# A recurrent layer on one core: the output projection of a turn by seven block products of 64 columns in place of eight, one turn later

## What is computed

```python
Xz = einsum('btc,hc->tbh', X, Wxz) + bxz      # the same for r and h
def step(H, xs):
    Z = sigmoid(xz + H @ Whz.T + bhz)
    R = sigmoid(xr + H @ Whr.T + bhr)
    H_tilda = tanh(xh + R * H @ Whh.T + bhh)
    H_new = Z * H + (1.0 - Z) * H_tilda
    return H_new, H_new @ Whq.T + bhq
out = x + transpose(Ys, (1, 0, 2))
```

## Time and profile before

| | us |
|---|---|
| median of 3 runs | 2182.04 (2181.3 to 2182.8) |
| the profiled execution | 2182.93 |
| its span | 2181.1 |
| PE busy | 2167.1 (99%) |
| DVE busy | 1544.8 (71%) |
| ACT busy | 788.2 (36%) |
| POOL busy | 173.1 (8%) |

### The profile page before, as it was taken

How to read it: one execution, slowest core, us unless ns; L and a number is a source line. 1 busy time by engine, 2 the same in 40 slices (tenths; PEclk the granted TensorE clock), 3 DMA queues, 4 the chain that set the end, 5 groups by cost and what they waited for, 6 DMA issues and landing times.

```text
span 2181.1 us, 180846 instructions
## 1 busy us (share of the span) xinstructions
PE 2167.1 (99%) x78920; PEld 2153.9 (99%) x78920; DVE 1544.8 (71%) x9602; ACT 788.2 (36%) x4611; POOL 173.1 (8%) x519
## 2 busy tenths in 40 slices
PE   8999999999999999999999999999999999999999
PEld 7999999999999999999999999999999999999998
DVE  5677777777777777777777777777777777777776
ACT  2333333333333333333333333333333333333333
POOL 2000000000000000000000000000000000000000
PEclk9999999999999999999999999999999999999999
DMA  4000000000000000000000000001000000000000
GB/s 163 24 27 25 25 25 27 25 25 25 27 25 25 25 26 25 25 25 24 27 24 26 23 28 23 26 23 28 23 26 23 28 23 26 23 28 24 26 23 24
DMA packets 112290, 62.68 MB, mean 29 GB/s; under 512 B 29328, under 2 KB 111376, under 8 KB 111504
## 3 DMA queue, kind: packets, MB, share of 16 engines
q1 hardware_dynamic: 112272, 62.41, 9.7%
HBM read 45.58 MB, written 16.78 MB: 29 GB/s over the span
## 4 chain that ended last, share of the span: by engine, by line
PE 98%; DMA 0%; DVE 0%; issue 0%; ACT 0%; SPq 0%; DVEq 0%
PE gates L307 61%; PE p_bank L272 17%; PE gates L272 11%; PE y_bank L281 10%; DMA wx_u<-in_w_xu 0%; DVE reset_state L568 0%; DVE pre_t L506 0%; DVE t L594 0%; DVE fresh L536 0%; ACT cand L491 0%; ACT r_gate L471 0%; DVE states L542 0%; ACT z_not L474 0%; DVE kept L577 0%; SPq L203 0%
## 5 line engine op out<-in xcount | busy, mean ns | idle before, releaser
L307 PE MATMUL gates<-wh,states 128*16 128x128 f32 x32768 | 1032.8, 273 | 3.9 <-DMA wh<-in_w_hz 2.8
L307 PEld LDWEIGHTS gates<-wh,states 128*16 128x16 f32 x32768 | 938.4, 103 | 12.5 <-DMA wh<-in_w_hz 3.0
L506 DVE STREAM_TRANSPOSE pre_t<-gates 128x32 f32<-128x32 f32 (+2 forms) x3584 | 617.6, 216 | 316.9 <-PE gates L307 275.5
L307 PE MATMUL gates<-wh,reset_state 128*16 128x128 f32 (+1 forms) x16384 | 585.2, 273 | 1.9 <-DVE reset_state L568 1.9
L471 ACT ACTIVATE r_gate<-pre_t 128x16 f32<-128x16 f32 (+1 forms) x1536 | 234.4, 215 | 869.1 <-DVE pre_t L506 869.1
L307 PEld LDWEIGHTS gates<-wh,reset_state 128*16 128x16 f32 (+1 forms) x16384 | 467.4, 103 | 3.4 <-issue 2.6
L272 PE MATMUL p_bank<-t,s 128*32 128x128 f32 (+1 forms) x8184 | 422.9, 287 | 0.0
L281 PE MATMUL y_bank<-wq,states 128*32 128x128 f32 x8192 | 326.2, 273 | 1.5 <-DVE states L542 1.5
L491 ACT ACTIVATE cand<-pre_t 128x16 f32<-128x16 f32 (+1 forms) x1536 | 234.4, 215 | 233.4 <-DVE pre_t L506 233.4
L281 PEld LDWEIGHTS y_bank<-wq,states 128*32 128x32 f32 x8192 | 277.2, 110 | 1.9 <-DVE states L542 1.8
L272 PEld LDWEIGHTS p_bank<-t,s 128*32 128x32 f32 x8184 | 271.1, 110 | 0.9
(11 more groups left out here) (43 smaller groups left out, 1017.0 us busy)
## 6 DMA issues: line engine op xcount, KB each, us to landing
xr<-in_x_t SPq DMA_DIRECT2D x128, 128.0 KB, 2.0
y_io<-in_x_res SPq DMA_DIRECT2D x256, 64.0 KB, 1.7
out<-y_io SPq DMA_DIRECT2D x256, 64.0 KB, 1.6
x_b<-in_x_t SPq DMA_DIRECT2D x128, 32.0 KB, 1.7
wx_v<-in_w_xv SPq DMA_DIRECT2D x1, 1536.0 KB, 6.5
wx_u<-in_w_xu SPq DMA_DIRECT2D x1, 1536.0 KB, 10.3
wh<-in_w_hr SPq DMA_DIRECT2D x1, 1024.0 KB, 11.7
wh<-in_w_hz SPq DMA_DIRECT2D x1, 1024.0 KB, 14.8
```

Of the source, the lines that this page charges most:

```text
L307: mm = nc.tensor.matmul(gate_rows(g, par, slice(Q * j, Q * j + rows)), of, w, start=False, stop=(m == G - 1), skip_group_check=True)
L506: nc.vector.transpose(flat(pre_t[g][:, a:b]), gate_part(g, par, a, b)).then_inc(done, 1)
```

## The change

The output projection of a turn's two pairs is done by seven block products q1 to q7 as well, two quads deep and 64 columns wide (14 quads of 64 columns in place of 8 of 128). They need both pairs of a turn, so they run a turn later, except q1 and q2, which take pair a alone. They need three more things:

- four sums of weights (`wq_sum`), made once by GpSimd in the first turn (`output_sums`);
- four sums of states (`h_sum`), made by DVE at the start of step 0 (`state_sums`);
- copies and sums between parts of `y_bank`, by ACT (`copy_q1`, the copy to `q16`, the copy of `q167`, `fill_q`) and by DVE (`put_y`).

Both `add_y` of the turn before now stand at the start of step 3. `put_va` moves behind Z's transposes, `sum_2`, `sum_3` and `sum_4` of GpSimd go behind `z_turned` in place of `state_ready`. Parts of p1, p5, p6 and p7 move between the gaps, so that each step has 768 columns behind H and 128 ahead of it. Nothing of SP's loop changes. The last turn projects directly, both pairs at its end.

```diff
+        Q16_AT, Q5_AT, Q7_AT, Y_AT = 0, YW, 2 * YW, (3 * YW, 3 * YW + P)
...
+                nc.gpsimd.tensor_tensor(t1, high[:, 0:half], low[:, 0:half], ALU.subtract).then_inc(yt_ready[0], 1)
+                pool.wait_ge(yt_ready[0], 1)
+                nc.gpsimd.tensor_tensor(t2, high[:, half:G], t1, ALU.subtract).then_inc(yt_ready[1], 1)
+                nc.gpsimd.tensor_tensor(t3, high[:, half:G], high[:, 0:half], ALU.subtract).then_inc(yt_ready[2], 1)
+                pool.wait_ge(yt_ready[1], 1)
+                nc.gpsimd.tensor_tensor(t4, low[:, half:G], t2, ALU.subtract).then_inc(yt_ready[3], 1)
...
                     sum_1(i + 1)
-                    pool.wait_ge(state_ready[N - 1], 4 * i + 3)
+                    pool.wait_ge(z_turned, 4 * i + 2)
                     sum_2(i + 1)
+                    pool.wait_ge(z_turned, 4 * i + 3)
+                    sum_3()
+                    pool.wait_ge(z_turned, 4 * i + 4)
                     sum_4(i + 1)
-                    pool.wait_ge(state_ready[N - 1], 4 * i + 4)
-                    sum_3()
...
+            def y_product(at, of, w):
+                for m in range(half):
                     for j in range(G):
+                        mm = nc.tensor.matmul(y_bank[Q * j:Q * (j + 1), at:at + YW], of(m), w(m, j), start=False,
+                                              stop=(m == half - 1), skip_group_check=True)
+                return mm
+            def state(par, part):
+                return lambda m: states[:, par, part * half + m, B:3 * B]
+            def state_sum(n):
+                return lambda m: h_sum[n][:, m, :]
+            def wq_part(part, col):
+                return lambda m, j: wq[:, part * half + m, P * j + col:P * j + col + YW]
+            def wq_of(n):
+                return lambda m, j: wq_sum[n - 1][:, m, YW * j:YW * (j + 1)]
+            def q1():
+                y_product(Q16_AT, state(0, 0), wq_part(0, 0)).then_inc(q1_done, 1)
+            def q2():
+                y_product(Y_AT[0], state(0, 1), wq_part(1, 0)).then_inc(q2_done, 1)
+            def q3():
+                y_product(Y_AT[0] + YW, state_sum(4), wq_part(1, YW)).then_inc(q34_done, 1)
+            def q4():
+                y_product(Y_AT[1], state(1, 1), wq_of(4))
+            def q5():
+                y_product(Q5_AT, state_sum(1), wq_of(1))
+            def q6():
+                y_product(Q16_AT, state_sum(2), wq_of(2)).then_inc(q6_done, 1)
+            def q7():
+                y_product(Q7_AT, state_sum(3), wq_of(3)).then_inc(q57_done, 1)
...
-                    pe.wait_ge(s3_ready, i + 1)
-                    p7(0, WIDE)
+                    pe.wait_ge(yt_ready[3], 1)
+                    pe.wait_ge(ys2_ready, i)
+                    q6()
                 recur(H, i, 0, first)
                 if first:
                     pe.wait_ge(s2_ready, 1)
...
                         p6(m, ALL)
                     pe.wait_ge(p5_filled, 1)
                     for m in range(half):
-                        mm = p5(m)
+                        mm = p5(m, ALL)
                     mm.then_inc(p56_done, 1)
-                    pe.wait_ge(s3_ready, 1)
                     pe.wait_ge(t_ready[2], 1)
-                    p7(0, WIDE)
-                p7(0, NARROW)
+                pe.wait_ge(s3_ready, i + 1)
+                p7(0, ALL)
                 p7(1, ALL).then_inc(p7_done, 1)
                 if not first:
-                    project_y(2 * i - 1, 1, 0, G)
-                recur(R, i, 1)
-                recur(Z, i, 1)
+                    pe.wait_ge(q16_copied, i)
+                    q5()
+                    q7()
                 if not last:
                     pe.wait_ge(xr_loaded, 16 * (i + 2))
                     if first:
                         pe.wait_ge(p16_copied, 1)
                     p1(0, WIDE)
+                recur(R, i, 1)
+                recur(Z, i, 1)
+                if not last:
+                    p1(0, NARROW)
+                    p1(1, NARROW)
                 recur(H, i, 1)
                 if not last:
-                    p1(0, NARROW)
-                    p1(1, ALL).then_inc(p1_done, 1)
+                    p1(1, WIDE).then_inc(p1_done, 1)
...
-                    p5(0)
+                    p5(0, ALL)
+                    p5(1, NARROW)
                 recur(R, i, 2)
                 recur(Z, i, 2)
+                if not first:
+                    if last:
+                        pe.wait_ge(yv_b_put, i)
+                    else:
+                        pe.wait_ge(q_filled, i + 1)
+                    q4()
+                recur(H, i, 2)
                 if not last:
                     pe.wait_ge(s2_ready, i + 2)
                     pe.wait_ge(va_put, i + 2)
-                    p6(0, WIDE)
-                recur(H, i, 2)
+                    p6(0, ALL)
+                    p6(1, ALL)
+                    p5(1, WIDE).then_inc(p56_done, 1)
+                if not first:
+                    pe.wait_ge(ys4_ready, i)
+                    q3()
                 if not last:
-                    p6(0, NARROW)
-                    p6(1, ALL)
-                    p5(1).then_inc(p56_done, 1)
-                if first:
-                    pe.wait_ge(wq_loaded, 2 * 16)
-                project_y(2 * i, 0, 0, G if last else G - 1)
+                    if first:
+                        pe.wait_ge(wq_loaded, 16)
+                        pe.wait_ge(q_filled, 1)
+                    q1()
                 recur(R, i, 3)
                 recur(Z, i, 3)
                 if not last:
                     p2(0, WIDE)
                 recur(H, i, 3)
-                if not last:
-                    project_y(2 * i, 0, G - 1, G)
+                if last:
+                    pe.wait_ge(y_filled, 2)
+                    project_y(0)
+                else:
                     pe.wait_ge(ua_put, i + 1)
...
+                    pe.wait_ge(yv_a_put, i + 1)
+                    q2()
...
-            def fill_y(k):
-                act.wait_ge(y_added, k)
-                nc.scalar.copy(y_bank[:, 0:P], bias_out[:]).then_inc(y_filled, 1)
+            def fill_q():
+                nc.scalar.copy(y_bank[:, 0:3 * YW], bias_q[:]).then_inc(q_filled, 1)
+            def copy_q1(i):
+                act.wait_ge(q1_done, i + 1)
+                nc.scalar.copy(y_bank[:, Y_AT[0]:Y_AT[0] + YW], y_bank[:, Q16_AT:Q16_AT + YW]).then_inc(yv_a_put, 1)
...
-                    elif c == 3 and not last:
-                        copy_p16(i + 1)
+                    elif c == 2:
+                        if first:
+                            act.wait_ge(bias_q_ready, 1)
+                        else:
+                            act.wait_ge(y_u_put, i)
+                            nc.scalar.copy(y_bank[:, Y_AT[1]:Y_AT[1] + YW], q167[:]).then_inc(yv_b_put, 1)
+                        if not last:
+                            fill_q()
+                    elif c == 3:
+                        if not last:
+                            copy_p16(i + 1)
+                        if not first:
+                            act.wait_ge(y_added, 2 * i)
+                        if not last:
+                            copy_q1(i)
+                        else:
+                            for par in range(2):
+                                nc.scalar.copy(y_bank[:, Y_AT[par]:Y_AT[par] + P], bias_out[:]).then_inc(y_filled, 1)
                     for h, (a, b) in enumerate(PARTS):
                         act.wait_ge(r_turned[h], t + 1)
                         nc.scalar.activation(r_gate[:, a:b], pre_t[R][:, a:b, mine], ACT.Sigmoid
...
                     nc.scalar.activation(z_gate[:], pre_t[Z][:, :, mine], ACT.Sigmoid).then_inc(z_ready, 1)
                     if c == 0 and not first:
-                        fill_y(2 * i - 1)
+                        act.wait_ge(q6_done, i)
+                        nc.scalar.copy(q16[:], y_bank[:, Q16_AT:Q16_AT + YW]).then_inc(q16_copied, 1)
                     elif c == 1 and not last:
                         act.wait_ge(ub_put, i + 1)
                         fill_p5()
-                    elif c == 2 and first:
-                        act.wait_ge(wq_loaded, 2 * 16)
-                        nc.scalar.copy(y_bank[:, 0:P], bias_out[:]).then_inc(y_filled, 1)
-                    elif c == 2:
-                        fill_y(2 * i)
-                    elif c == 3 and last:
-                        fill_y(pairs - 1)
...
-            def add_y(k, par, loads):
+            def add_y(par, loads):
                 dve.wait_ge(y_loaded[par], 16 * loads)
-                dve.wait_ge(y_projected, k + 1)
-                nc.vector.tensor_tensor(y_io[:, par, :], y_bank[:, 0:P], y_io[:, par, :], ALU.add
+                nc.vector.tensor_tensor(y_io[:, par, :], y_bank[:, Y_AT[par]:Y_AT[par] + P], y_io[:, par, :], ALU.add
                                         ).then_inc(y_added, 1)
+            def state_sums(i):
```

(74 more changed lines are left out.)

28 lines of the change are left out of this document (16 added, 12 removed).

## The result

The changed kernel takes 2194.81 us (median of 5 runs, 2192.53 to 2196.78), the kernel before 2182.04 in the same rounds: a ratio of 1.0056, 95% interval 1.0045 to 1.0068. It is slower by 12.8 us; the forecast was 25. The profiled execution took 2192.81 us, 9.9 more than that of before.

A forecast was written before the change was run, and what follows sets the result against it. It took PE to bound the kernel before, and a new 17.01 us ring through SP's queue to bound the changed one: 2182.93 + 125 x 0.20 + 0.3 = 2208.2 profiled, so 2207 us; 8-in-10 range 2188 to 2228.

The forecast's parts named there:

- the ring: Waits from R3 through SP's queue, `xr` and p1 to the next R3: 17.01 us against 16.81, +0.20 a turn; chance 0.66.
- A: Rival: `xr` comes in time, PE does not wait; 2165 us, between 2159 and 2171; chance 0.14.
- B: Rival: narrow quads in a row on PE cost up to 0.218 each; turn 18.3 us, 2371 us; chance 0.04.
- C: Rival: same ring but longer, by a later first store or longer landings; 2230 to 2243 us; 0.14 together with D.
- D: Rival: gates' chain delays steps 1 and 2, +0.1 to 0.2 a turn; 2220 to 2232 us; 0.14 together with C.
- step 3: In SP's queue, residual load to `x_b` and `x_b` to second store, nothing to wait for: 0.62 us each.
- Products: On PE, 14 quads of 64 replace 8 of 128: turn 16.81 - 0.183 = 16.63 us, -23 us over 126 turns.
- Quad of 64: On PE, a quad of 64 columns takes 0.11 us, with bounds 0.107 and 0.218.
- Gaps: All steps have 768 columns behind H; steps 1 and 2 lose 0.11 of 0.15 us to spare; cost 0.
- `state_sums`: On DVE in step 0, four sums make R0's transposes late by 0.1 us; 0.05 a turn taken if PE sets it.
- Ends: First turn, GpSimd's weight sums and the last output's residual load with two stores at the end: together about +0.3 us.
- The signs to look for: Profile after: PE idle about 0.4 us ahead of `p1(0, WIDE)`, busy 97 or 98%, turn 17.0, R1 to R3 8.3.

The follow-up runs named there:

- x1: The changed kernel with the load of `x_b` moved right behind the load of `xr` in SP's queue: 2162.73 us, ratio 0.9913.
- x3: The changed kernel with `p1(0, WIDE)` and its wait for `xr` put back between Z1 and H1: 2177.53 us, ratio 0.9977.
- x2: The changed kernel with one more 32 KB load a turn, which nobody reads, ahead of the second store: 2261.39 us, ratio 1.0364.
- x4: The kernel before with p1 and p5 cut and placed as in the change, without the products: 2183.95 us, ratio 1.0007.
- x7: The kernel before with only the load of `x_b` moved next to that of `xr` in SP's queue: 2182.7 us, ratio 1.0.
- x5: The kernel before with each quad of the output projection cut into two of 64 columns: 2190.57 us, ratio 1.0037.
- x6: The changed kernel with `x_b`'s load next to `xr`'s and both stores ahead of both residual loads: 2162.06 us, ratio 0.9911.

## Why the prediction was right and wrong

**The direction and the mechanism were right.** A new wait for `xr` ahead of `p1(0, WIDE)`, a ring R3, stores, loads, `xr`, p1, R1, R3 that is longer than PE's own turn. x1 and x3 take the wait away from either side, the queue's and PE's, and x2 lengthens the ring, and the turn follows. x3 and x4 show that neither of the change's two moves makes the wait alone, and x7 that the order of the queue is worth nothing where PE sets the turn. The rivals: A (no wait) did not hold, though its place at "8.27" was near; B fell in x5; C fell, the ring is shorter than taken, though the first store is issued 0.09 later than taken, as C has it; D fell, steps 1 and 2 have H to R at 2.188 us, like the others, in x1 without the ring.

**What failed is the size of the ring**, its step 3. The terms from R3 to p1, means over 90 turns of the changed kernel's trace, beside the prediction's:

| step | forecast | measured |
|---|---|---|
| 1. R3 to first store | 0.80 | 0.886 |
| 2. store to residual load | 1.72 | 1.708 |
| 3. residual load to `x_b` | 0.62 | 0.517 |
| 3. `x_b` to second store | 0.62 | 0.517 |
| 4. store to residual load | 1.72 | 1.741 |
| 5. residual load to `xr` | 0.96 | 0.896 |
| 6. `xr` issue to landing | 1.93 | 2.006 |
| 6. landing to PE | 0.10 | 0.043 |
| sum, R3 to p1 | 8.47 | 8.314 |
| p1 to R1 | 0.22 | 0.243 |
| R1 to R3 | 8.32 | 8.317 |
| ring | 17.01 | 16.87 |

PE alone reaches p1 8.09 after R3 (8.10 in x1: 1004.01 to 1012.11), so its wait is 0.22 to 0.24 a turn and not 0.38. The other six terms up to p1 are off by up to 0.09 and nearly cancel: +0.09, -0.01, +0.02, -0.06, +0.08, -0.06, together +0.05. "0.62" is wrong twice in the same direction, -0.21, and leaves the sum 0.16 too long. Of the others, the first is later because `add_y` starts 0.23 behind q1's end where 0.13 was taken from the last turn of before, and the landing of `xr` was put at 1.93 against the 2.0 of the earlier trace rows without a row for it.

The prediction said of it: "nothing to wait for: 0.62, as between the two issues at 1001.06 and 1001.68 or at 1009.14 and 1009.76". The second pair did wait. Its own rows say so: `add_y` ended at 1009.32 + 0.28 = 1009.60, and step 1 of the same sum used the 0.16 from there to 1009.76 as the time from `add_y` to its store. A row can't be the length of a wait in one term and of free issuing in another. In x4 the same pair is 0.84 apart (1009.89 and 1010.73), the second again 0.16 behind the end of `add_y` (1010.57); and in x7 the second store, with nothing to wait for, follows the issue ahead of it by 0.52. The first pair, 1001.06 and 1001.68, was no wait for `add_y` (over at 1001.41). It was issued freely, but with one register operation of SP more between the issues than the pairs at 0.52 have. x7 has that operation too, ahead of its first store, and 0.63 there. So 0.62 is read rightly from the first pair, but for another sequence of instructions than that of step 3. No run separated the register operation from the rest.

**What was luck.** With 0.52 twice the sum would have been 8.27 to p1, the very point at which the prediction's rival A says that it "costs as much as it gives": a forecast of no change, where the kernel is slower by 12.8. Steps 1 and 6 (issue to landing) were taken too short, by 0.09 and 0.08, and the error of step 3 made up for them. The mechanism was found by reasoning; that the sum came out on the slow side is owed to the error of step 3. And the ring's error, 0.14 a turn, is 17 us of the kernel; that the forecast is off by only 12 comes from the terms below that were no part of its sum.

**Why so small a term weighs so much.** 0.2 us a turn was the difference of 17.01 and 16.81, and a term of 0.1 that stands twice in the ring is 25 us of the kernel. The bounds given (16 us for all terms together) cover the 12 by which the forecast is off, but not quite the ring's own 17. Of the 12.8 us, the profiles show 9.5 in their spans: 126 turns of +0.058 are 7.3; the loop's first iteration is 1.1 (it takes 2.6 more than the median turn in the change, 1.5 before) and other turns near the loop's two ends some 0.6; the first turn 0.3 (the loop's first R0 at 41.16, before at 40.87); R0 to R3 of the last turn -0.4, and from there to the end +0.6. The remaining 3.3 are the medians' distance to the profiled executions (2.0 above it in the change, 0.9 below it before) and 0.4 outside the spans. The change's runs spread over 4.3 us and before's over 1.8. The ring contains six issues and three landings. In the trace the second store's landing and that of `xr` vary by 0.05 (standard deviation) and the turn by 0.07, where the turns of before and of x1 are all alike. That would make the spread, but the runs in question have no trace.

**Point by point.** *Products*: right, 16.63 for PE alone, seen in x1 and x6 (16.628). *Quad of 64*: right, 0.111 in x5. *Gaps*: right that they cost nothing, and with more to spare than the "0.05 us" at 768 columns, which was right for the kernel before. In x1 the first part of the state is written at 1012.15 and R1 starts at 1012.32, and with 640 columns (x3) R1 comes 0.06 behind that write:

```profile
1018.58 0.17 DVE L683 TENSOR_TENSOR states<-fresh,kept 128x16 f32<-128x16 f32 x1
```

1018.75 to 1018.81. So 768 columns have 0.11 to spare. The chain from H0 to that write takes 2.01 us in the change, x1 and x3, and 2.07 before, in each of the four steps; no run shows why. *`state_sums`*: the steps were right, the 0.05 was not needed. The fourth sum starts 1.09 behind R0 and the transposes 1.23 (before: 1.19 in each step; in steps 1 to 3 of the change 1.12). R0 to H0 is 1.970, as for the other steps, in x1 too where PE sets the turn. So the sums do make step 0 late by 0.1, as forecast, but against steps that have become shorter:

```profile
1005.83 0.23 DVE L639 TENSOR_TENSOR ys<-states 128x64 f32<-128x64 f32 x1 [0.28 <-DVE states L684]
...
1006.49 0.23 DVE L644 TENSOR_TENSOR ys<-states,ys 128x64 f32<-128x64 f32 x1
1006.63 0.44 DVE L626 STREAM_TRANSPOSE pre_t<-gates 128x32 f32<-128x32 f32 x3
```

Rival A was therefore priced too dear: without the wait the kernel is at 2162.7 (x1), at the fast end of "between 2159 and 2171". *ACT and GpSimd*: right, nothing on PE waits for them in steady turns. *Ends*: +0.3 forecast for them; without the first iteration of the loop, which was not in the sum, they are +0.5. The last output waits for its residual load as described:

```profile
2188.29 0.29 DVE L630 TENSOR_TENSOR y_io<-y_bank,y_io 128x128 f32<-128x128 f32 x1 [0.51 <-DMA y_io<-in_x_res]
```

*The signs to look for*: PE's busy share at "97 or 98%" was wrong, it reads 99%, since matmul rows overlap: that of q5 and q7 above ends at 1009.52, behind the start of p1 at 1009.45, and so covers the wait; SP's issues do lie between R3 and 2.1 us behind R0, and R1 to R3 is 8.32.

## What to carry to other kernels

When a wait is moved earlier and its releaser later, close the ring: from the waiting instruction through the queues back to itself, and compare its length with the turn of the busiest engine; what makes the ring shorter than the turn (here a 32 KB load issued elsewhere in the same queue) is free. Give each term of the ring from a row in which that very thing was free to go, and test the row: look at what each issue could have waited for before taking its pitch. When ring and turn differ by a per cent, the sum can tell the mechanism and where to cut, but hardly the sign, and the chances should say so: here 0.83 for slower stood on 0.20 us in 17.

## What the runs showed that was not expected

- How far apart SP issues DMAs with nothing to wait for depends on the instructions between them: 0.52 us as a rule, 0.62 with one register operation more, 0.39 for the spare load of x2, which has none of its own, and 0.90 over the end of the loop. A store's issue through its landing to the next dependent issue is 1.70 to 1.77 us, also where a second store follows at once (x6: 1.70); it is 1.90 for the first store of the kernel before, with a load of `xr` just ahead of it.
- On SP's queue loads of 32 KB (`x_b`, the spare load) land 1.70 to 1.85 us after their issue, residual loads of 64 KB mostly after 1.75, and loads of 128 KB (`xr`) after 2.0. The Trainium skill (DMA: Bandwidth & Descriptors, Anatomy of one DMA) gives a fixed cost of about 2.0 us and the data's time on top, for DMAs that GpSimd issues. The loads here come from SP, and the smaller ones stay below it.
- The first iteration of the loop is longer than the rest by 1.0 to 3.1 us, other in each of nine profiles (before 1.5, x4 1.0, x2 1.3, x5 3.1). In those of before and of the change its rows show PE idle for 0.2 to 0.4 us at a time with no releaser. Between two kernels that is up to 2 us, where x3 differs from before by 5.
- Cutting a quad in two costs 0.005 us: eight quads of 128 columns in x5, two of 192 in x4.
